# Decoder layer on one Trainium2 core: two output banks for the down projections, and two silus ahead of the turned rows of tile 4

## The chip, the cores and the metric

One Trainium2 chip, one core of it. The metric is the device time of one execution of the whole program in microseconds (us); the time before is the median of three runs. The engines are called PE (TensorE, with PEld for its weight loads), ACT (ScalarE), DVE (VectorE), POOL (GpSimd) and SP (SyncE, which here only issues transfers).

## The reference, cut to what matters

The layer is causal self attention, differential cross attention and a feed-forward part, each behind a layer norm and added to the residual x. The change lies in the last part alone:

```python
def bit_linear(x, w):                      # rows of x in 255 steps, w in three values
    xq = x + stop_gradient(act_quant(x) - x)
    wq = w + stop_gradient(weight_quant(w) - w)
    return einsum('bsd,hd->bsh', xq, wq)
h = bit_linear(x, w1)                      # 128 -> 512
h = depthwise_conv1d(h, conv_w, conv_b)    # 3 taps along the tokens
h = silu(h)
return bit_linear(h, w2)                   # 512 -> 128
```

`act_quant` takes the largest absolute value of a token's row, scales the row to 127 by it, and rounds. So the second `bit_linear` can't begin for a token before the whole row of 512 hidden values is there. x is 2 x 512 tokens of 128 float32 values.

## The kernel before

The 1024 tokens are 8 tiles of 128 (`TT` = 8; four to a batch row). The program is written out by hand, engine by engine: each engine has its own list of instructions, and semaphores carry all order between engines. An engine that stands at a wait holds up all that is behind it in its list.

In the feed-forward part each tile i goes through these steps, each on its engine:

- `conv(i)` on PE (line 984): 10 matmuls of 512 columns, up projection and convolution in one, into one of four banks of PSUM (`CONV_BANK`). A PSUM bank holds 512 float32 values per partition.
- `silu(i)` on ACT (line 665): bank to `hs[:, i % 2]`. It waits for `conv(i)` and, from tile 2 on, until tile i-2 is quantised out of the same half of `hs` (`hq_done`).
- `hidden_scale(i)` on DVE (line 1684): the row's largest value `hmax`, then two small operations to the scale. Three instructions, each waiting for the one before.
- `quantise_hidden(i)` on POOL (line 467) for tiles 0 to 6; for tile 7 `quantise_last` on DVE (line 1693): `hs` times the scale, rounded, into `hq[:, i % 2]`, and then a small operation on the tile's factor `hdq`.
- `turn_hidden(i)` on PE (line 1001): four 128x128 transposes into `HIDDEN_BANK[i % 2]`.
- `turned_hidden(i)` on ACT (line 671): that bank to `hiT[:, i % 2]` in bfloat16. It waits for `turn_hidden(i)` and, from tile 2 on, for `down(i - 2)`, which reads the same half of `hiT`.
- `down(i)` on PE (line 1018): four matmuls of 128 columns into columns 0 to 127 of bank `OB` (bank 7). All eight tiles use this one bank, so `down(i)` waits until `finish(i - 1)` has read it (`f_done` at i).
- `finish(i)` on DVE (line 1702): bank `OB` times `hdq`, plus `x_sb`, into `x_sb`.
- SP (line 285) stores each tile to `out` when it is finished.

The lists around the change, in short. PE (lines 1248 to 1258): ..., `down(1)`, `turn_hidden(2)`, `conv(6)`, `down(2)`, `turn_hidden(3)`, `conv(7)`, `turn_hidden(4)`, `down(3)`, `turn_hidden(5)`, `down(4)`, `turn_hidden(6)`, `down(5)`, `turn_hidden(7)`, `down(6)`, `down(7)`. ACT (lines 712 to 716): `silu(4)`, turned rows of tile 2, `silu(5)`, turned rows 3, `silu(6)`, turned rows 4, `silu(7)`, turned rows 5, 6, 7. DVE (lines 1719 to 1724): `finish(0)`, `hidden_scale(4)`, ..., `finish(3)`, `hidden_scale(7)`, `quantise_last`, `finish(4)`, `finish(5)`, `finish(6)`, `finish(7)`. POOL has the seven `quantise_hidden` in order.

Bank `PJ0` (bank 0) is used earlier in this part for turning the normed tokens; its last reader there is DVE's `low_ints(3, 1, ...)` (line 1716), which counts `xdTl_done` to 3.

In the profile every matmul made by the helper `mm` has line 721. `conv` shows there as `bank<-qk,wqk_h` and the like (the weights lie in `qk`, the tokens in `wqk_h` and `wqk_l`), `down` as `bank<-w_q,pT`, transposes of `turn_hidden` as `bank<-con,onT` at line 1014. `hs` and `hq` show as `onT`, `hiT` as `pT`, because they share that memory.

Of the kernel before, what the change touches and what calls it, by code (L numbers as in the profile page):

```python
# [13 lines left out]
P = 128  # L14
B, T, C = 2, 512, 128
H, DH = 16, 64
NT = T // P
TT = B * NT
# [32 lines left out]
PJ0, SM, PJ1, ST0, ST1, OB = 0, 1, 3, 5, 6, 7  # L51
# [2 lines left out]
VB = (PT, PT + 1, OB)  # L54
CONV_BANK = (PT, PT + 1, SM, SM + 1)
HIDDEN_BANK = (ST0, ST1)
OUT_BANK = (ST1, ST0)
ATT_BANK = (PJ0, OB)

# [21 lines left out]
def decoder_layer(nc, x, consts, wqk, wv, wo, ctxT, xwq, xbq, xwk, xbk, xwv, xbv, xwo, xbo, lam_in,  # L81
                  w1, cw, cb, w2, out):
    with ExitStack() as ctx:
        def sb(name, shape, dt=F32):
            return ctx.enter_context(nc.sbuf_tensor(name, shape, dt))
# [4 lines left out]
        bank = ctx.enter_context(nc.psum_tensor("bank", [P, 8, 512], F32))  # L90


        x_sb = sb("x_sb", [P, TT, C])
# [54 lines left out]
        w2_q = sb("w2_q", [P, FH // P, C], BF16)  # L148
# [10 lines left out]
        hdq = sb("hdq", [P, TT])  # L159
# [40 lines left out]

        xq, cb_row = places(kb_[:, :, :, :].rearrange("p a b c -> p (a b c)"), (NT, C), (FH,))
        _, hiT_f = places(pT_flat, (2, FH // 2), (2, FH // 2))
        hiT, cb_sb = hiT_f.bitcast(BF16), cb_row[0:2]
        qf = onT[:, 6:8, :]
# [15 lines left out]
        def sem_names(*names):  # L220
            return [sem(n) for n in names]
# [27 lines left out]
        wcs, xdTl_done, hq_done, xb_done = sem_names("wcs", "xdTl_done", "hq_done", "xb_done")  # L249
        xd_done, xdT_ps, xdT_done, conv_ps, silu_done, hsc_done, hiT_ps, hiT_done, f_ps, f_done = sem_names(  # L250
            "xd_done", "xdT_ps", "xdT_done", "conv_ps", "silu_done", "hsc_done", "hiT_ps", "hiT_done", "f_ps",
            "f_done")
# [243 lines left out]
        def _(act):  # L496
# [168 lines left out]
            def silu(i):  # L665
                act.wait_ge(conv_ps, i + 1)
                if i >= 2:
                    act.wait_ge(hq_done, i - 1)
                nc.scalar.activation(hs[:, i % 2, :], bank[:, CONV_BANK[i % 4], :], ACT.Silu).then_inc(silu_done, 1)

            def turned_hidden(i):

                act.wait_ge(hiT_ps, i + 1)
                if i >= 2:
                    act.wait_ge(f_ps, i - 1)
                nc.scalar.activation(hiT[:, i % 2, :], bank[:, HIDDEN_BANK[i % 2], :], ACT.Identity,
                                     bias=minus_round[:, :]).then_inc(hiT_done, 1)
# [31 lines left out]
            turned_ints(3, 1, halves[1])  # L709
            silu(3)  # L710
            turned_hidden(1)
            for i in range(4, TT):
                silu(i)
                turned_hidden(i - 2)
            turned_hidden(TT - 2)
            turned_hidden(TT - 1)

        @block.tensor
        def _(pe):
            def mm(out_, lhsT, rhs, start, stop, **kw):  # L720
                return nc.tensor.matmul(out_, lhsT, rhs, start=start, stop=stop, **kw)  # L721
# [249 lines left out]
            def cross_out(at, ts, done):  # L971
                for t in ts:
                    last = mm(bank[:, at, C * t:C * t + C], attT[:, t * P:t * P + P], xwo_sb[:, :], t == ts[0],
                              t == ts[-1], skip_group_check=True)
                last.then_inc(done, 1)
# [8 lines left out]
            def conv(i, taps=range(3)):  # L984

                b, t = i // NT, i % NT
                o = bank[:, CONV_BANK[i % 4], :]
                if taps[0] == 0:
                    pe.wait_ge(xdTl_done, 1 if b == 0 else 2 if t == 0 else 3)
                    if i in (0, 2):  # L990
                        pe.wait_ge(round_done, part_sums + 1 + i // 2)
                    if i >= 4:
                        pe.wait_ge(silu_done, i - 3)
                    mm(o, ones_row[0:2, :], cb_h[0:2], True, False)
                for k in taps:
                    cols = slice(t * P + k, t * P + k + P)
                    last = mm3(o, xdT_h[:, b, cols], xdT_l[:, b, cols], wc_h[:, k, :], wc_l[:, k, :], False, k == 2)
                if taps[-1] == 2:
                    last.then_inc(conv_ps, 1)

            def turn_hidden(i):
# [8 lines left out]
                else:  # L1010
                    pe.wait_ge(hiT_done, i - 1)
                o = bank[:, HIDDEN_BANK[i % 2], :]
                for k in range(FH // P):
# [4 lines left out]
            def down(i):  # L1018
                pe.wait_ge(hiT_done, i + 1)
                if i == 0:  # L1020
                    pe.wait_ge(xo_done, 2)
                else:
                    pe.wait_ge(f_done, i)
                for k in range(FH // P):
                    last = mm(bank[:, OB, 0:C], hiT[:, i % 2, k * P:k * P + P], w2_q[:, k, :], k == 0,
                              k == FH // P - 1)
                last.then_inc(f_ps, 1)

# [206 lines left out]
            pe.wait_ge(attT_done, 2)  # L1235
            cross_out(OUT_BANK[0], first, xo_ps)
            pe.wait_ge(attT_done, 3)
            cross_out(OUT_BANK[1], second, xo_ps)
            conv(1, [1, 2])
# [6 lines left out]
            conv(4, [1, 2])  # L1246
            turn_ints(1, second)
            down(0)
            turn_hidden(1)
            conv(5)  # L1250
            for i in range(6, TT):
                down(i - 5)
                turn_hidden(i - 4)
                conv(i)
            for i in range(TT - 4, TT):
                turn_hidden(i)
                down(i - 1)
# [3 lines left out]
        def _(dve):  # L1261
# [290 lines left out]
            def cross_residual(b, h=0):  # L1552
# [3 lines left out]
                else:  # L1556
                    dve.wait_ge(xo_ps, h + 1)
                    at, ts, n = OUT_BANK[h], range(HALF * h, HALF * h + HALF), HALF
                xs = x_sb[:, NT * b + ts[0]:NT * b + ts[-1] + 1, :]
# [142 lines left out]
            def finish(i):  # L1702
                if i + 1 < TT:
                    dve.wait_ge(hdq_done, i + 1)
                dve.wait_ge(f_ps, i + 1)
                nc.vector.scalar_tensor_tensor(x_sb[:, i, :], bank[:, OB, 0:C], hdq[:, i:i + 1],
                                               x_sb[:, i, :], ALU.mult, ALU.add).then_inc(f_done, 1)

            hidden_scale(0)
# [9 lines left out]
            for i in range(4, TT):  # L1719
                finish(i - 4)  # L1720
                hidden_scale(i)
            quantise_last()
            for i in range(TT - 4, TT):
                finish(i)
# [104 lines left out]
```

## Time and profile before

| | us |
|---|---|
| median of 3 runs | 322.48 |
| the three runs | 322.57, 322.48, 315.58 |
| the profiled execution, its own time | 317.07 |
| its span, first to last instruction | 314.2 |
| time outside the span | 2.87 |
| granted PE clock, mean over the span | 0.989 of full |
| PE busy | 283.5 (90%) |
| DVE busy | 219.8 (70%) |
| ACT busy | 195.1 (62%) |
| POOL busy | 143.1 (46%) |

All positions in time below are us from the start of the span. A row of the timeline gives start, duration, engine, line, operation, what is written and read, and in brackets how long the engine had been idle and what released it. Ends of matmuls are modelled. Engines start an instruction a little before the one in front has drained, so starts can be closer together than durations.

### The profile page before, as it was taken

The page shows a single profiled execution, that of the slowest core. Times are in us where ns is not written, and L with a number is a line of the kernel's source. Part 1 is how long each engine was busy: PE and PEld are TensorE (multiplying, and loading weights), DVE is VectorE, ACT ScalarE, POOL GpSimd, SP SyncE. Part 2 cuts the span into 40 slices and gives each one's busy share as a digit, 9 for nine tenths or more (in the row PEclk, how much of TensorE's full clock was granted, in tenths as well). Part 3 has the DMA queues.
Part 4 walks back from the last instruction along what each step waited for, and adds up shares of the span by engine and source line. Part 5 has one row for each costly group of instructions (what it writes and reads, how often), then busy time and mean ns, then how long its engine had stood idle before and what let it go on. Part 6 is the DMA issues. An engine that isn't in the chain of part 4 may idle for free.

```text
span 314.2 us, 6619 instructions
## 1 busy us (share of the span) xinstructions
PE 283.5 (90%) x2446; PEld 179.3 (57%) x2446; DVE 219.8 (70%) x481; ACT 195.1 (62%) x484; POOL 143.1 (46%) x252
## 2 busy tenths in 40 slices
PE   0899699899999989989899999999999988898893
PEld 0567556566666668656566677445445443355672
DVE  3777767896776642869566747988888689527834
ACT  2588467668777760886677820778867866534333
POOL 3523767794477762565465500086326208001320
PEclk9999889999999999999999999999999999999997
DMA  7920000000000000000000000000000000000001
GB/s 273 306 87 3 0 3 1 2 2 0 3 2 3 2 0 2 0 3 0 2 2 3 2 2 0 2 0 0 2 0 3 1 0 3 0 2 0 8 17 42
DMA packets 4834, 6.16 MB, mean 20 GB/s; under 512 B 834, under 2 KB 3650, under 8 KB 4676
## 3 DMA queue, kind: packets, MB, share of 16 engines
q1 hardware_dynamic: 4516, 5.42, 4.9%
q10 hardware_dynamic: 288, 0.33, 0.4%
q8 instruction: 19, 0.31, 0.4%
q14 instruction: 11, 0.09, 0.1%
HBM read 5.23 MB, written 0.52 MB: 18 GB/s over the span
## 4 chain that ended last, share of the span: by engine, by line
PE 67%; DVE 19%; ACT 7%; issue 5%; DMA 1%; POOL 1%; ACTq 0%; DVEq 0%; POOLq 0%
PE bank L721 58%; PE bank L794 5%; ACT pr L545 4%; DVE nmax L1343 3%; DVE qk L1388 3%; DVE xn L1287 1%; DMA x_sb<-in_x 1%; ACT pT L545 1%; DVE stats L1274 1%; PE bank L946 1%; PE bank L848 1%; DVE qs L1323 1%; PE bank L1014 1%; DVE xn L1669 1%; DVE pT L1359 1%
## 5 line engine op out<-in xcount | busy, mean ns | idle before, releaser
L645 ACT ACTIVATE pT<-bank 128x512 f32<-128x512 f32 (+1 forms) x80 | 44.5, 600 | 25.6 <-PE bank L721 25.1
L338 POOL TENSOR_SCALAR pr<-pr,pinv 128x256 f32<-128x256 f32 (+2 forms) x96 | 45.5, 492 | 29.7 <-DVE pinv L1351 29.6
L1388 DVE TENSOR_REDUCE qk<-bank 128x4 fp32r<-128x616 f32 x64 | 49.0, 796 | 13.6 <-PE bank L721 13.4
L545 ACT ACTIVATE pr<-bank,nmax 128x256 f32<-128x256 f32 (+2 forms) x96 | 44.4, 480 | 18.2 <-DVE nmax L1343 17.9
L721 PE MATMUL bank<-qs 64*128 64x256 f32 (+3 forms) x256 | 50.4, 477 | 4.1 <-ACT pr L545 3.8
L1343 DVE TENSOR_REDUCE nmax<-bank 128x2 f32<-128x512 f32 (+2 forms) x48 | 31.6, 687 | 14.5 <-PE bank L721 14.5
L721 PE MATMUL bank<-pT,v_sb 128*64 128x128 f32 (+2 forms) x320 | 38.4, 385 | 0.0
L338 POOL TENSOR_SCALAR pT<-pT,pinv 128x512 f32<-128x512 f32 x32 | 21.8, 693 | 23.9 <-DVE pinv L1351 23.9
L1359 DVE COPY pT<-bank 128x512 f32<-128x512 f32 (+1 forms) x32 | 30.4, 949 | 1.6 <-PE bank L794 1.5
L721 PEld LDWEIGHTS bank<-pT,v_sb 128*64 128x64 f32 x320 | 21.1, 136 | 14.1 <-issue 10.8
L721 PE MATMUL bank<-km,qk 64*128 64x308 f32 x128 | 27.7, 366 | 1.2 <-DVE qk L1388 1.1
L721 PE MATMUL bank<-qk,km 64*128 64x512 f32 x64 | 27.2, 438 | 1.2 <-ACT pT L645 1.2
L721 PEld LDWEIGHTS bank<-qs 64*128 64x128 f32 x256 | 19.8, 189 | 8.5 <-ACT pr L545 4.3
L348 POOL TENSOR_TENSOR km<-kb_,con 128x1232 fp32r<-128x1232 f32 x8 | 17.9, 2244 | 13.5 <-PE bank L721 13.5
L1351 DVE RECIPROCAL pinv<-psum 128x2 f32<-128x2 f32 x64 | 10.0, 160 | 19.2 <-ACT pT L545 12.8
L721 PEld LDWEIGHTS bank<-mask_b,sel_b 64*128 64x128 bf16 x256 | 13.2, 95 | 17.5 <-issue 13.2
L545 ACT ACTIVATE pT<-bank,nmax 128x512 f32<-128x512 f32 x32 | 22.2, 695 | 1.0 <-DVE nmax L1337 1.0
L556 ACT COPY pT<-bank 128x512 f32<-128x512 f32 x32 | 17.2, 590 | 6.9 <-PE bank L794 6.9
L1337 DVE TENSOR_REDUCE nmax<-bank 128x1 f32<-128x512 f32 x32 | 20.4, 680 | 1.2 <-PE bank L721 1.2
L721 PEld LDWEIGHTS bank<-km,qk 64*128 64x128 f32 x128 | 13.9, 184 | 11.4 <-DVE qk L1388 7.4
L545 ACT ACTIVATION_READ_ACCUMULATOR pr<-bank,nmax 128x1 f32 x96 | 20.2, 211 | 0.0
L473 POOL TENSOR_SCALAR onT<-onT,hscale 128x512 f32<-128x512 f32 x7 | 4.9, 695 | 32.8 <-DVE hscale L1691 26.7
(190 smaller groups left out, 578.9 us busy)
## 6 DMA issues: line engine op xcount, KB each, us to landing
pT<-in_wqk SPq DMA_DIRECT2D x1, 1024.0 KB, 6.3
cw_sb<-in_cw SPq DMA_DIRECT2D x1, 768.0 KB, 8.8
x_sb<-in_x SPq DMA_DIRECT2D x2, 256.0 KB, 5.5
pT<-in_wv SPq DMA_DIRECT2D x1, 512.0 KB, 7.1
wo_sb<-in_wo SPq DMA_DIRECT2D x1, 512.0 KB, 7.3
out<-x_sb SPq DMA_DIRECT2D x8, 64.0 KB, 1.5
onT<-in_consts ACTq DMA_DIRECT2D x1, 256.0 KB, 5.0
pT<-in_xwk SPq DMA_DIRECT2D x1, 256.0 KB, 7.5
```

The lines of the kernel that those rows point to most:

```text
L338: nc.gpsimd.tensor_scalar(d, d, pinv[:, t, a:a + 1], 1.0, ALU.mult, ALU.mult).then_inc(norm_done, 1)
L348: nc.gpsimd.tensor_tensor(km[:, g, :, :], _repeat(kb_[:, g, b, :], GP), _bcast(con[:, C_ROWM:C_ROWM + GP], S2), ALU.mult).then_inc(km_done, 1)
L545: nc.scalar.activation(prob[r][:, a, at:at + w], bank[:, SP[k % 2] + a, at:at + w], ACT.Exp, bias=nmax[:, t, a:a + 1], accum_out=psum[:, t ...
L556: nc.scalar.copy(turned_to(1, 2 * NT)[:, half], bank[:, at, :].rearrange("p (m q) -> p m q", q=64)).then_inc(pt_act, 1)
L645: nc.scalar.activation(px[rows, i, :], bank[rows, (ST0, ST1)[i % 2], :], ACT.Exp, scale=SD ** -0.5).then_inc(xexp_done, 1)
L721: return nc.tensor.matmul(out_, lhsT, rhs, start=start, stop=stop, **kw)
L794: last = nc.tensor.transpose(bank[:, to, at:at + 64], prob[r][own, a, P * i:P * i + P], con[own, C_ID + 64 * half:C_ID + 64 * half + 64])
L1337: nc.vector.tensor_reduce(nmax[:, NT - 1, a:a + 1], bank[:, SP[k % 2] + a, :], AX.X, ALU.max, negate=True).then_inc(max_done, 1)
L1343: nc.vector.tensor_reduce(nmax[:, t, :], bank[:, SP[k % 2]:SP[k % 2] + 2, at:at + w], AX.X, ALU.max, negate=True).then_inc(max_done, 1)
L1351: nc.vector.reciprocal(pinv[:, t, :], psum[:, t, :]).then_inc(inv_done, 1)
L1359: nc.vector.tensor_copy(turned_to(slot, blocks), turned_from(PT, PT + 2, blocks)).then_inc(pt_dve, 1)
L1388: nc.vector.tensor_reduce(m, s_in, AX.X, ALU.max, negate=True).then_inc(round_done, 1)
```

## The change

`down(i)` writes, and `finish(i)` reads, `DOWN_BANK[i % 2]`: bank `OB` for even tiles and bank `PJ0` for odd ones. With two banks `down(i)` waits for `finish(i - 2)` (`f_done` at i - 1) instead of `finish(i - 1)`; `down(1)`, the first in `PJ0`, waits for the bank's last earlier reader (`xdTl_done` at 3). On ACT the last tiles are reordered: `silu(6)` and `silu(7)` are issued one behind the other, and the turned rows of tile 4, which stood between them, come after both. No instruction is added or taken away.

```diff
+DOWN_BANK = (OB, PJ0)
...
-            for i in range(4, TT):
+            for i in range(4, TT - 2):
                 silu(i)
                 turned_hidden(i - 2)
-            turned_hidden(TT - 2)
-            turned_hidden(TT - 1)
+            silu(TT - 2)
+            silu(TT - 1)
+            for i in range(TT - 4, TT):
+                turned_hidden(i)
...
                 pe.wait_ge(hiT_done, i + 1)
                 if i == 0:
                     pe.wait_ge(xo_done, 2)
+                elif i == 1:
+                    pe.wait_ge(xdTl_done, 3)
                 else:
-                    pe.wait_ge(f_done, i)
+                    pe.wait_ge(f_done, i - 1)
                 for k in range(FH // P):
-                    last = mm(bank[:, OB, 0:C], hiT[:, i % 2, k * P:k * P + P], w2_q[:, k, :], k == 0,
+                    last = mm(bank[:, DOWN_BANK[i % 2], 0:C], hiT[:, i % 2, k * P:k * P + P], w2_q[:, k, :], k == 0,
                               k == FH // P - 1)
...
                 dve.wait_ge(f_ps, i + 1)
-                nc.vector.scalar_tensor_tensor(x_sb[:, i, :], bank[:, OB, 0:C], hdq[:, i:i + 1],
+                nc.vector.scalar_tensor_tensor(x_sb[:, i, :], bank[:, DOWN_BANK[i % 2], 0:C], hdq[:, i:i + 1],
                                                x_sb[:, i, :], ALU.mult, ALU.add).then_inc(f_done, 1)
```

ACT's list before, from `silu(4)` (here `onT<-bank`; `pT<-bank,minus_round` are the turned rows, the first of them here tile 2's) to the end of the program:

```order
L669 ACTIVATE onT<-bank 128x512 [waits hq_done,conv_ps]
L676 ACTIVATE pT<-bank,minus_round 128x512 [waits f_ps,hiT_ps]
L669 ACTIVATE onT<-bank 128x512 [waits hq_done,conv_ps]
L676 ACTIVATE pT<-bank,minus_round 128x512 [waits f_ps,hiT_ps]
L669 ACTIVATE onT<-bank 128x512 [waits hq_done,conv_ps]
L676 ACTIVATE pT<-bank,minus_round 128x512 [waits f_ps,hiT_ps]
L669 ACTIVATE onT<-bank 128x512 [waits hq_done,conv_ps]
L676 ACTIVATE pT<-bank,minus_round 128x512 [waits f_ps,hiT_ps] x3
```

And the same list after the change, from `silu(4)` to the end:

```order
L670 ACTIVATE onT<-bank 128x512 [waits hq_done,conv_ps]
L677 ACTIVATE pT<-bank,minus_round 128x512 [waits f_ps,hiT_ps]
L670 ACTIVATE onT<-bank 128x512 [waits hq_done,conv_ps]
L677 ACTIVATE pT<-bank,minus_round 128x512 [waits f_ps,hiT_ps]
L670 ACTIVATE onT<-bank 128x512 [waits hq_done,conv_ps] x2
L677 ACTIVATE pT<-bank,minus_round 128x512 [waits f_ps,hiT_ps] x4
```

`silu(7)` has moved ahead of one instruction, the turned rows of tile 4; everything before and behind stays. The lists of PE, DVE, POOL and SP hold the same instructions in the same order and wait for the same semaphores (but for `down(1)`, which waited for `f_done`); only the values waited for and the bank differ.

## Rows read from the trace of the kernel before

**Rows 1.** The page, granted PE clock in 40 slices, in tenths of full.

```profile
PEclk9999889999999999999999999999999999999997
```

**Rows 2.** Busy time by stretch; the number behind PEld to POOL's is the granted clock.

```profile
302.64:306.00 3.36, 3.36 (x20) 2.67 (x20) 1.09 (x4) 1.29 (x3) 0.93 (x2) 1.00 0.07 20
306.00:310.00 4.00, 2.00 (x22) 1.51 (x19) 2.48 (x8) 2.23 (x4) 0.93 (x2) 1.00 0.06 16
310.00:312.30 2.30, 1.14 (x10) 0.58 (x8) 0.89 (x3) 0.69 (x1) 0.00 (x0) 0.64 0.29 84
```

**Rows 3.** The chain that ended last, in order of time: start, us, what.

```profile
308.85 0.36 DVE x_sb L1706
309.21 0.14 issue
309.34 0.40 PE bank L721 x4
...
309.83 0.36 DVE x_sb L1706
```

**Rows 4.** Timeline of PE from the last matmul of conv(7).

```profile
305.01 0.40 PE L721 MATMUL bank<-qk,wqk_h 128*128 128x512 f32 x1
305.25 0.60 PE L1014 MATMUL bank<-con,onT 128*128 128x128 f32 x4
305.69 0.39 PE L721 MATMUL bank<-w_q,pT 128*128 128x128 bf16 x4
305.91 0.61 PE L1014 MATMUL bank<-con,onT 128*128 128x128 f32 x4
306.68 0.38 PE L721 MATMUL bank<-w_q,pT 128*128 128x128 bf16 x4 [0.16 <-ACT pT L676]
306.90 0.61 PE L1014 MATMUL bank<-con,onT 128*128 128x128 f32 x4
...
309.56 0.61 PE L1014 MATMUL bank<-con,onT 128*128 128x128 f32 x4
...
311.32 0.58 PE L721 MATMUL bank<-w_q,pT 128*128 128x128 bf16 x4 [0.60 <-DVE x_sb L1706]
```

**Rows 5.** Timeline of ACT, same stretch.

```profile
305.89 0.69 ACT L676 ACTIVATE pT<-bank,minus_round 128x512 bf16<-128x512 f32 x1 [1.96 <-PE bank L1014]
306.47 0.59 ACT L669 ACTIVATE onT<-bank 128x512 f32<-128x512 f32 x1
306.95 1.28 ACT L676 ACTIVATE pT<-bank,minus_round 128x512 bf16<-128x512 f32 x2
310.21 0.69 ACT L676 ACTIVATE pT<-bank,minus_round 128x512 bf16<-128x512 f32 x1 [1.98 <-PE bank L1014]
```

**Rows 6.** Timeline of DVE: hidden_scale(4), then the end of the program.

```profile
297.60 0.69 DVE L1687 TENSOR_REDUCE hmax<-onT 128x1 f32<-128x512 f32 x1 [0.28 <-ACT onT L669]
...
306.18 0.35 DVE L1706 SCALAR_TENSOR_TENSOR x_sb<-bank,hdq,x_sb 128x128 f32<-128x128 f32 x1 [1.15 <-PE bank L721]
307.10 0.69 DVE L1687 TENSOR_REDUCE hmax<-onT 128x1 f32<-128x512 f32 x1 [0.56 <-ACT onT L669]
...
308.20 0.49 DVE L1697 TENSOR_SCALAR onT<-onT,hscale 128x512 f32<-128x512 f32 x1
...
311.94 0.35 DVE L1706 SCALAR_TENSOR_TENSOR x_sb<-bank,hdq,x_sb 128x128 f32<-128x128 f32 x1 [0.77 <-PE bank L721]
```

**Rows 7.** Timeline of POOL: tiles 3, 5 and 6 quantised.

```profile
297.15 0.69 POOL L473 TENSOR_SCALAR onT<-onT,hscale 128x512 f32<-128x512 f32 x1
...
302.88 0.69 POOL L473 TENSOR_SCALAR onT<-onT,hscale 128x512 f32<-128x512 f32 x1 [2.44 <-PE bank L1014]
...
306.02 0.69 POOL L473 TENSOR_SCALAR onT<-onT,hscale 128x512 f32<-128x512 f32 x1 [2.20 <-PE bank L1014]
```

**Rows 8.** The page, transfers out: count, KB each, median us to landing.

```profile
out<-x_sb SPq DMA_DIRECT2D x8, 64.0 KB, 1.5
```

## The prediction

> **What bounds the kernel now.** I read the stretches first, then the chain of waits from its end backwards, then the engines' timelines beside it. Up to 306 the feed-forward part is bound by PE: the stretch that holds `conv(7)` is 3.36 us long and PE is busy for all of it at the full clock [rows 2]. Nothing that ACT or DVE does there ends last, so neither half of the change can gain there. From 306.00 to 310.00 PE is busy for 2.00 us of 4.00, and from 310.00 to 312.30 for 1.14 of 2.30 [rows 2]: the end of the program is a chain of short steps that hand over between engines. In that chain stands the pattern this change is about. `finish(4)` runs on DVE at 308.85, PE's `down(5)` starts 0.14 us behind its end, at 309.34, and `finish(5)` follows at 309.83 [rows 3]. The same happens for tiles 6 and 7, up to `down(7)` at 311.32 and `finish(7)` at 311.94 [rows 4, 6]. One bank is written, read, written, read. Worse, `turn_hidden(7)` stands behind `down(5)` in PE's list: its input was quantised at 308.20 + 0.49 = 308.69 [rows 6], yet it starts at 309.56 [rows 4]. What leads to 308.85 is tile 7's own path: `silu(7)` at 306.47 [rows 5], `hmax` of tile 7 at 307.10 and the quantising at 308.20 [rows 6].
>
> **The silus, step by step.** In before, `silu(7)` starts at 306.47, 0.58 behind the turned rows of tile 4 at 305.89, for which ACT had waited 1.96 us [rows 5]. Its own inputs were ready: the last matmul of `conv(7)` runs from 305.01 to 305.41 [rows 4], and tile 5 was quantised out of that half of `hs` by 302.88 + 0.69 = 303.57 [rows 7]. So now `silu(7)` starts at about 305.45, a microsecond earlier, and ends at 306.04. Not all of that counts. DVE's list has `finish(3)` ahead of tile 7's `hmax`, and it starts at 306.18 because `down(3)` stands at 305.69 behind `turn_hidden(4)` [rows 4, 6]; nothing in the change moves it. It lasts 0.35, so `hmax` starts at 306.53 in place of 307.10: 0.57 us gained, with 0.45 of the silu's lead lost to the queue on DVE. If DVE overlaps its drain with the next start, as ACT does, it could be 0.05 to 0.1 more. The following steps keep their distance of 1.10 from `hmax` to quantising [rows 6]: quantising starts at 307.63 and ends at 308.12.
>
> What the moved silu costs: the turned rows of tile 4 stand behind it now. An activation behind a silu starts 0.48 later (306.47 to 306.95, rows 5), so they start at 305.93 instead of 305.89. That is 0.04 late, and `down(4)` with `turn_hidden(6)` move by the same to 306.72 and 306.94 [rows 4]. Had the silu's start been 0.3 later than I think, `down(4)` would be 0.3 later, and still nothing that ends last would be touched, since `turn_hidden(6)` and `down(5)` have until 308.1. POOL's quantising of tile 6 waits for `turn_hidden(4)` and stays at 306.02 [rows 7]. It will now lie beside tile 7's `hmax`. The trace has that pair already: `hmax` of tile 4 at 297.60 took 0.69 with POOL's quantising at 297.15 beside it, and tile 7's at 307.10 took 0.69 with POOL idle [rows 6, 7]. I take nothing for it.
>
> **The banks, step by step.** Until 306 every `down(i)` found `finish(i - 1)` long done, so the looser wait gives nothing. `down(5)` now needs `finish(3)` (done at 306.53) and the turned rows of tile 5 (start 305.93 + 0.58 = 306.51, end about 307.20). It starts right behind `turn_hidden(6)`, 0.44 after it as `down(3)` does behind `turn_hidden(4)` [rows 4]: 307.38, done before 307.8. PE then stands free at `turn_hidden(7)`, which starts when DVE has quantised tile 7. With the 0.14 us that PE took behind DVE [rows 3], that is 308.12 + 0.14 = 308.26. From there by the distances of before: turned rows of tile 7 on ACT 0.65 later (309.56 to 310.21, rows 4 and 5), 308.91; `down(7)` 0.79 behind them (305.89 to 306.68, rows 4 and 5), 309.70; `finish(7)` 0.49 behind that (309.34 to 309.83, rows 3), 310.19. In between nothing is later: `finish(4)` stands 0.65 behind the start of the quantising (308.20 to 308.85, rows 3 and 6), at 308.28, and ends at 308.63; `down(6)` needs that and starts at 308.77; `finish(5)` at about 308.6; `finish(6)` at 309.26 to 309.61. All are out of the way of 309.70.
>
> **The sum.** `finish(7)` at 310.19 in place of 311.94: 1.75 us. Of this the silus alone give 0.57 (the whole chain behind `hmax` shifts). The banks alone give 1.18: quantising ends at 308.69, so 308.83, 309.48, 310.27, 310.76 by the same steps. The four last stores now come at about 0.3, 0.65 and 0.95 us from each other instead of 1 us. A store of 64 KB lands in 1.5 us [rows 8] and the last has its nearest neighbour 0.9 us ahead, so I take the 2.3 us behind `finish(7)` as unchanged; if the transfers did queue, it would cost some tenths. Bounds: PE behind DVE at 0.04 instead of 0.14, `hmax` 0.08 earlier and so on give 1.95. The clock gives the other end. In before it had fallen when `down(7)` ran: 0.64 of full on average in that stretch, and 0.58 us for four matmuls that took 0.38 before [rows 2, 4]. I count the full clock for the new `down(7)`, because it comes at 309.70, before the stretch in which the clock fell; if it is at 1.2 GHz there and in `turn_hidden(7)`, I lose 0.2 to 0.4. So 1.35 to 1.95, with 1.75 taken.
>
> Against the profiled execution: 317.07 - 1.75 = 315.3, or 0.55%. That execution lay near the lowest of the three runs (315.58); the median is 322.48, and the same step from it gives 320.7. The profile does not tell what makes 322 out of 316. About 2% is what a measurement of this kernel can tell from no change, and the three runs alone differ by 7 us, so I expect a real gain that a comparison by 2% calls the same.
>
> **The rivals.** *The silus give nothing* (gain 1.2, 321.3). The ends of matmuls are modelled; if the semaphore of `conv(7)` shows only at about 305.9, or DVE's queue holds tile 7's `hmax` until POOL is through with tile 6's rows at 306.71, the banks' share is left. For it: `silu(7)`'s lead is partly eaten already. Against it: the pair of `hmax` and POOL above.
>
> *The banks give nothing* (gain 0.6, 321.9). That needs something else to hold `turn_hidden(7)` or `down(5)`: the half of `hiT`, or the hidden bank. By rows both are free by 307.3.
>
> *The clock falls in the stage and the kernel ends slower.* PE is the bound until 305.4, and each us of its full-speed work done at 1.2 GHz instead of 2.4 costs up to another us. The clock stands in the highest tenth in every slice from the middle of the program to the last, is at 1.00 up to 310, and fell only at the end, behind a PE that had stood idle from 307.51 to 309.34 and in short pieces since [rows 1 to 4]. If the change made it fall at the first `down` in the second bank, `down(1)`, two rounds of 3.36 us are left up to the end of `conv(7)`: up to 6.7 us more, 1.75 less, so +5.0 and 327.4. It turns the sign from 1.75 us of such work on. Nothing in the rows speaks for it, since PE has the same instructions back to back there and no gap is added. The Trainium skill, page "TensorE: Matmul & The Clock Gate", section "A second HAM failure mode: psum-queue depth-cycling", reports a kernel in which cycling through PSUM banks on each iteration made the engine idle briefly between groups of matmuls and the clock go up and down. By that rule a second bank for `down` could bring this rival about. Convolutions and turned rows here cycle through six banks in that stage already, with the clock at 1.00 [rows 2], so the trace speaks against it here, and I leave it a small chance.
>
> *The measurement lands elsewhere.* If the median falls to the lower of the two levels seen, it reads 315.58 - 1.75 = 313.8, over 2% below 322.48, with the same 1.75 us of real gain.
>
> **How the numbers follow.** Forecast 0.77; silus nothing 0.10; banks nothing 0.05; clock 0.04; other level of the median 0.04. Within 2% are the first three and half of the clock's case, which at +1.6% lies just inside: 0.94. Faster by more is the other level, 0.04; slower by more the other half of the clock's case, 0.02. The range runs from 313.5 (the lowest run less the gain, with its upper bound) to 322.5 (the median without any gain). It is that wide because of the runs, not of the sum; the sum's own range about the median is 320.5 to 321.1.
>
> **What would show it.** Right: `silu(7)` near 305.45 and directly behind it the turned rows of tile 4; tile 7's `hmax` at 306.5 directly behind `finish(3)`; `down(5)` near 307.4 with no wait for DVE; `turn_hidden(7)` released by DVE's quantising at 308.1 to 308.3; `down(7)` released by ACT and not by DVE; span 312.4 to 312.5. Wrong: `down(5)` or `down(6)` still ahead of the path, `hmax` of tile 7 longer than 0.69, or a clock below full before 308.

## The result, and the profile after

| | before | changed |
|---|---|---|
| median of 19 runs, us | 316.62 | 314.47 |
| lowest, us | 315.53 | 313.19 |
| profiled execution, us | 317.07 | 314.22 |
| its span, us | 314.2 | 312.3 |
| PE busy, us | 283.5 | 283.3 |
| first `turn_hidden(4)` to start of `finish(7)`, us | 6.69 | 4.71 |

The ratio is 0.9937, with a 95% interval of 0.991 to 0.9964: some 2.0 us gained (1.1 to 2.8), a real step that is the same kernel by a bound of 2%. Some executions of either kernel (5 of 19 before, 3 of 19 after) take 320 us or more, the changed kernel's at a mean clock of 0.97 instead of 0.98 to 1.00; two of the three runs shown ahead of the prediction were such, and the ratio leaves them out. Of the 2.85 us between the two profiled executions 1.9 lie inside the span; the rest is time outside it (2.87 before, 1.92 after), and no part of what the change does.

The stretches of the changed kernel answer to [rows 2]:

```profile
302.64:306.00 3.36, 3.36 (x21) 2.63 (x20) 1.13 (x4) 1.69 (x4) 0.94 (x2) 1.00 0.07 20
306.00:310.00 4.00, 3.00 (x30) 2.07 (x28) 2.84 (x10) 2.65 (x5) 0.94 (x2) 1.00 0.13 37
310.00:312.30 2.30, 0.00 (x0) 0.00 (x0) 0.35 (x1) 0.00 (x0) 0.00 (x0) 1.00 0.27 78
```

The stage bound by PE is as it was: busy for all of its 3.36 us at clock 1.00. From 306 to 310 PE now does 3.00 us of work instead of 2.00, and behind 310 it has nothing left.

The timeline of PE, against [rows 4]:

```profile
305.29 0.60 PE L1017 MATMUL bank<-con,onT 128*128 128x128 f32 x4
305.72 0.39 PE L724 MATMUL bank<-w_q,pT 128*128 128x128 bf16 x4
305.94 0.61 PE L1017 MATMUL bank<-con,onT 128*128 128x128 f32 x4
306.72 0.40 PE L724 MATMUL bank<-w_q,pT 128*128 128x128 bf16 x4 [0.17 <-ACT pT L677]
306.95 0.61 PE L1017 MATMUL bank<-con,onT 128*128 128x128 f32 x4
307.39 0.39 PE L724 MATMUL bank<-w_q,pT 128*128 128x128 bf16 x4
308.12 0.66 PE L1017 MATMUL bank<-con,onT 128*128 128x128 f32 x4 [0.34 <-DVE onT L1702]
308.73 0.38 PE L724 MATMUL bank<-w_q,pT 128*128 128x128 bf16 x4
309.56 0.40 PE L724 MATMUL bank<-w_q,pT 128*128 128x128 bf16 x4 [0.45 <-ACT pT L677]
```

`down(5)` at 307.39 waits for nothing; before, it stood at 309.34 with 1.84 us of idle PE ahead of it, put down to `finish(4)`:

```profile
309.34 0.38 PE L721 MATMUL bank<-w_q,pT 128*128 128x128 bf16 x4 [1.84 <-DVE x_sb L1706]
```

`turn_hidden(7)` at 308.12 is released by DVE's quantising, and `down(7)` at 309.56 by ACT: no row of PE is released by a finish any more. The timelines of ACT and of DVE, against [rows 5, 6]:

```profile
305.49 0.60 ACT L670 ACTIVATE onT<-bank 128x512 f32<-128x512 f32 x1 [1.52 <-PE bank L724]
305.98 1.30 ACT L677 ACTIVATE pT<-bank,minus_round 128x512 bf16<-128x512 f32 x2
307.59 0.69 ACT L677 ACTIVATE pT<-bank,minus_round 128x512 bf16<-128x512 f32 x1 [0.32 <-PE bank L1017]
308.82 0.69 ACT L677 ACTIVATE pT<-bank,minus_round 128x512 bf16<-128x512 f32 x1 [0.54 <-PE bank L1017]
```

```profile
306.22 0.35 DVE L1711 SCALAR_TENSOR_TENSOR x_sb<-bank,hdq,x_sb 128x128 f32<-128x128 f32 x1 [1.14 <-PE bank L724]
306.48 0.68 DVE L1692 TENSOR_REDUCE hmax<-onT 128x1 f32<-128x512 f32 x1
...
307.58 0.49 DVE L1702 TENSOR_SCALAR onT<-onT,hscale 128x512 f32<-128x512 f32 x1
...
308.23 0.61 DVE L1711 SCALAR_TENSOR_TENSOR x_sb<-bank,hdq,x_sb 128x128 f32<-128x128 f32 x2
...
310.00 0.35 DVE L1711 SCALAR_TENSOR_TENSOR x_sb<-bank,hdq,x_sb 128x128 f32<-128x128 f32 x1 [0.43 <-PE bank L724]
```

`silu(7)` stands at 305.49, directly ahead of the turned rows of tiles 4 and 5. `hmax` of tile 7 has no idle time ahead of it: it starts right behind `finish(3)`. `finish(4)` and `finish(5)` have become one row of two, where [rows 3] had a `down` between them.

### The profile page after: what moved, and what is told of

Same layout as the page of the kernel before. It is cut to its first block, busy times and chain, and to the rows that moved or that the text cites. A ratio compares the mean times of both kernels' runs of the same rounds, so it can differ in the third digit from the quotient of the medians.

```text
span 312.3 us, 6619 instructions
## 1 busy us (share of the span) xinstructions
PE 283.3 (91%) x2446; PEld 179.2 (57%) x2446; DVE 219.7 (70%) x481; ACT 195.2 (63%) x484; POOL 143.5 (46%) x252
## 4 chain that ended last, share of the span: by engine, by line
PE 67%; DVE 18%; ACT 7%; issue 5%; DMA 1%; POOL 1%; ACTq 0%; DVEq 0%; POOLq 0%
PE bank L724 58%; PE bank L797 5%; ACT pr L546 4%; DVE nmax L1348 3%; DVE qk L1393 3%; DVE xn L1292 1%; DMA x_sb<-in_x 1%; ACT pT L546 1%; DVE stats L1279 1%; PE bank L949 1%; PE bank L1017 1%; PE bank L851 1%; DVE qs L1328 1%; DVE xn L1674 1%; DVE pT L1364 1%
```

## The experiments

The part ahead of the tail differs from execution to execution: `turn_hidden(4)` started anywhere from 304.30 to 305.41 in the ten profiles. So spans of single profiles can't be compared to tenths. I compare the tail, which leaves out that part: from the start of `turn_hidden(4)` to the start of `finish(7)`.

### One half of the change at a time

First run: the banks and the looser wait, with ACT's list as before.

```diff
-            for i in range(4, TT - 2):
+            for i in range(4, TT):
                 silu(i)
                 turned_hidden(i - 2)
-            silu(TT - 2)
-            silu(TT - 1)
-            for i in range(TT - 4, TT):
-                turned_hidden(i)
+            turned_hidden(TT - 2)
+            turned_hidden(TT - 1)
```

> Two banks for the down projections and the looser wait, ScalarE's list as before. Theory (the chain as predicted, with the distances of the changed kernel): hmax of tile 7 stays at 307.10 and its quantising at 308.20, but turn_hidden(7) follows it at once at about 308.73 instead of 309.56; from the quantising's start to finish(7) it is 2.42 us as in the changed kernel, so finish(7) at 310.6 and a span of 312.9, 1.3 us below before (314.2). Rival (the banks do nothing, all of the gain is the silus' order): finish(7) at 311.9, span 314.2.

Second run: the kernel before with ACT's new list, one bank and the old wait.

> One bank and the old wait, ScalarE's last two silus ahead of the turned rows of tile 4. Theory: hmax of tile 7 at 306.48 directly behind finish(3), 0.62 earlier than before, the whole ladder of finish and down behind it shifts by that: down(5) at 308.7 behind finish(4), finish(7) at 311.3, span 313.6, a gain of 0.6 us. If the granted clock stays at full there, down(7) takes 0.4 instead of 0.58 and it is 0.8. Rival (the silus' order gives nothing, or gives its whole 1.0 us): span 314.2, or 313.2.

Banks alone, timeline of PE:

```profile
304.30 0.60 PE L1015 MATMUL bank<-con,onT 128*128 128x128 f32 x4
...
306.75 0.40 PE L722 MATMUL bank<-w_q,pT 128*128 128x128 bf16 x4 [0.23 <-ACT pT L677]
307.80 0.66 PE L1015 MATMUL bank<-con,onT 128*128 128x128 f32 x4 [0.66 <-DVE onT L1700]
308.40 0.38 PE L722 MATMUL bank<-w_q,pT 128*128 128x128 bf16 x4
309.23 0.40 PE L722 MATMUL bank<-w_q,pT 128*128 128x128 bf16 x4 [0.45 <-ACT pT L677]
```

Silus alone, timeline of PE:

```profile
304.93 0.60 PE L1016 MATMUL bank<-con,onT 128*128 128x128 f32 x4
...
308.37 0.38 PE L723 MATMUL bank<-w_q,pT 128*128 128x128 bf16 x4 [1.17 <-DVE x_sb L1708]
308.59 0.61 PE L1016 MATMUL bank<-con,onT 128*128 128x128 f32 x4
309.35 0.38 PE L723 MATMUL bank<-w_q,pT 128*128 128x128 bf16 x4 [0.16 <-DVE x_sb L1708]
310.34 0.38 PE L723 MATMUL bank<-w_q,pT 128*128 128x128 bf16 x4 [0.60 <-DVE x_sb L1708]
```

With the banks alone the waits of PE name ACT and the quantising, and no finish; `finish(7)` starts at 309.67, a tail of 5.37 us. With the silus alone the ladder is still there, each `down` released by a finish (`DVE x_sb`), only earlier; `finish(7)` starts at 310.76, a tail of 5.83 us. The two starts of `finish(7)`, from the timelines of DVE, banks alone and silus alone:

```profile
309.67 0.35 DVE L1709 SCALAR_TENSOR_TENSOR x_sb<-bank,hdq,x_sb 128x128 f32<-128x128 f32 x1 [0.43 <-PE bank L722]
310.76 0.35 DVE L1708 SCALAR_TENSOR_TENSOR x_sb<-bank,hdq,x_sb 128x128 f32<-128x128 f32 x1 [0.57 <-PE bank L723]
```

The whole runs agree in order: 0.9955 (0.9941 to 0.9969) for the banks, 0.9974 (0.9952 to 0.9996) for the silus, which lies only just clear of no change. Both halves gain; the rivals by which one does nothing are out.

### Two banks with the old wait

```diff
-                elif i == 1:
-                    pe.wait_ge(xdTl_done, 3)
                 else:
-                    pe.wait_ge(f_done, i - 1)
+                    if i == 1:
+                        pe.wait_ge(xdTl_done, 3)
+                    pe.wait_ge(f_done, i)
```

> The changed kernel with two banks and both silus ahead, but down(i) waits again for finish(i-1). Theory (the wait carries the gain, not the bank that is written beside the one that is read): as the silus alone, finish(7) at 311.3, span 313.6. Rival (a bank of its own speeds the pair of writer and reader by itself): finish(7) near 310.0 and a span near 312.3 as in the changed kernel, or matmuls and finishes shorter than 0.38 and 0.35.

```profile
305.00 0.60 PE L1017 MATMUL bank<-con,onT 128*128 128x128 f32 x4
...
308.44 0.38 PE L724 MATMUL bank<-w_q,pT 128*128 128x128 bf16 x4 [1.17 <-DVE x_sb L1711]
...
310.42 0.58 PE L724 MATMUL bank<-w_q,pT 128*128 128x128 bf16 x4 [0.60 <-DVE x_sb L1711]
```

This timeline of PE has the ladder of the silus alone, number by number: 3.44 us from `turn_hidden(4)` to `down(5)` in both. Its tail is 6.04 us (`finish(7)` at 311.04), 0.21 more than with one bank, and the last row holds that: `down(7)` took 0.58 instead of 0.38, since the granted clock was 0.58 from 310 to 311 in this execution and 1.00 in the other. The finish took 0.35 us in both. So a bank of its own is worth nothing by itself; it is the permission not to wait. The ratio to before is 1.0002 (0.9975 to 1.0029). That holds no change and the expected span of 313.6 alike (0.6 us less, some 0.998), so the whole runs don't show here what the silus still give; but all of the interval lies above the changed kernel's (0.991 to 0.9964).

### The queue on DVE, and the clock

The prediction had the silu's lead partly eaten by `finish(3)`, which stands ahead of tile 7's `hmax` in DVE's list. To move `finish(3)` behind the quantising, `down(5)` must not wait for it. So the last four down projections got the banks that their own tile's convolution had left:

```diff
-DOWN_BANK = (OB, PJ0)
+DOWN_BANK = (OB, PJ0, OB, PJ0, PT, PT + 1, SM, SM + 1)
...
-                else:
+                elif i < 4:
                     pe.wait_ge(f_done, i - 1)
+                else:
+                    pe.wait_ge(silu_done, i + 1)
...
                                         ALU.add).then_inc(hq_last, 1)
+                finish(TT - 5)
...
-            for i in range(4, TT):
+            for i in range(4, TT - 1):
                 finish(i - 4)
                 hidden_scale(i)
+            hidden_scale(TT - 1)
             quantise_last()
```

> On top of the change: the last four down projections each write the bank that their own tile's convolution has left, so that they wait for no finish, and on VectorE finish(3) goes behind the quantising of tile 7. Theory (VectorE's queue eats 0.4 us of the silu's lead): hmax of tile 7 starts behind its silu at 306.12 instead of 306.48, quantising at 307.22, turn_hidden(7) at 307.8 right behind down(5), finish(7) at 309.65, span 311.95, 0.35 us below the changed kernel. Rival (POOL or PE's own queue gates tile 7): hmax earlier but turn_hidden(7) still at 308.1 and the span at 312.3.

Its timeline of DVE:

```profile
305.17 0.69 DVE L1694 TENSOR_REDUCE hmax<-onT 128x1 f32<-128x512 f32 x1 [1.04 <-ACT onT L670]
...
306.27 0.48 DVE L1704 TENSOR_SCALAR onT<-onT,hscale 128x512 f32<-128x512 f32 x1
306.68 0.34 DVE L1714 SCALAR_TENSOR_TENSOR x_sb<-bank,hdq,x_sb 128x128 f32<-128x128 f32 x1
...
308.69 0.35 DVE L1714 SCALAR_TENSOR_TENSOR x_sb<-bank,hdq,x_sb 128x128 f32<-128x128 f32 x1 [0.45 <-PE bank L724]
```

`hmax` is now released by the silu (`ACT onT`) and the finish comes behind the quantising. `turn_hidden(4)` stood at 304.33, so the tail is 4.36 us: 0.35 less than the changed kernel, as expected. The ratio to before is 0.9933 (0.9909 to 0.9958). Four more runs, two of them timed side by side and two of one execution each (own banks, and the kernel before):

> The changed kernel with the last four down projections each in the bank that their own tile's convolution has left, VectorE's list as in the changed kernel. Theory (with two banks no down projection of the tail waits for a finish any more): nothing moves, 4.7 us from the first of turn_hidden(4) to the start of finish(7), as in the changed kernel. Rival (a finish still gates down(5) or down(6)): below 4.6 us.

Tail 4.72 us (305.39 to 310.11), against 4.71 in the changed kernel. Own banks alone move nothing; the 0.35 us are the order on DVE: `hmax` of tile 7 starts 0.84 us behind `turn_hidden(4)` with the late finish, 1.19 in the changed kernel and 1.20 with own banks alone.

> The changed kernel once more, on the same chip as the next run. Theory: 4.7 us from turn_hidden(4) to finish(7), whatever the part ahead of it does; ratio to before 0.993 to 0.995. Rival (the fall of the clock at the end belongs to the kernel before alone): the granted clock stays at 1.00 to the end. By the theory that the clock falls or not from run to run, either can be seen.

> Own banks and finish(3) behind the quantising of tile 7, once more beside the changed kernel. Theory: 4.35 us from turn_hidden(4) to finish(7), 0.35 us less than the changed kernel, so a ratio to before lower by 0.001. Rival: no difference of medians that the rounds can tell, since the part ahead of the tail varies by more.

Tails 4.71 us (304.79 to 309.50) and 4.36 us (305.41 to 309.77): both repeat to 0.01 us. The ratios to before are 0.9895 (0.9845 to 0.9945) and 0.9895 (0.984 to 0.9951): the rounds can't tell the two apart. For the changed kernel 0.993 to 0.995 was expected, so the ratio missed. The medians, 314.17 and 314.32, are where the changed kernel lay before (314.47); what pulls both ratios down and makes the intervals twice as wide is the kernel before in these rounds: the seven executions of it that they rest on are scattered from 315.67 to 319.68. The version with the late finish has the shorter tail in both of its profiles, but in the time of the whole kernel its lead is not shown.

> The kernel before once more. Theory: 6.7 us from turn_hidden(4) to finish(7) if the clock falls again before down(7), 6.5 if it stays at full, since down(7) then takes 0.38 instead of 0.58. Rival (the fall is fixed by the work ahead of it): the clock falls at the same place, near 310.7, in this execution too.

The kernel before, once more, timeline of PE:

```profile
304.95 0.60 PE L1014 MATMUL bank<-con,onT 128*128 128x128 f32 x4
...
309.04 0.38 PE L721 MATMUL bank<-w_q,pT 128*128 128x128 bf16 x4 [1.84 <-DVE x_sb L1706]
...
311.02 0.38 PE L721 MATMUL bank<-w_q,pT 128*128 128x128 bf16 x4 [0.60 <-DVE x_sb L1706]
```

Here the same `down(7)` takes 0.38 us and `finish(7)` starts at 311.44, a tail of 6.49 us. The start of `finish(7)`, from its timeline of DVE:

```profile
311.44 0.35 DVE L1706 SCALAR_TENSOR_TENSOR x_sb<-bank,hdq,x_sb 128x128 f32<-128x128 f32 x1 [0.57 <-PE bank L721]
```

The clock's fall at the end, 0.2 us in [rows 4], belongs to the execution and not to the kernel: PE stood idle for the same 1.84 us in both. The changed kernel's two profiles had it at 1.00 to the end. The late finish had it at 1.00 in one profile, and in the other at 0.68 from 310.00 to 312.30, when PE had ended its work at 309.73 and nothing was lost by it.

All tails together, in us:

| kernel | tail | tail at full clock |
|---|---|---|
| before | 6.69 and 6.49 | 6.49 |
| silus alone | 5.83 | 5.83 |
| two banks, old wait, silus | 6.04 | 5.84 |
| banks alone | 5.37 | 5.37 |
| changed | 4.71 and 4.71 | 4.71 |
| own banks | 4.72 | 4.72 |
| own banks, late finish | 4.36 and 4.36 | 4.36 |

(5.84 is 6.04 less the 0.20 that `down(7)` took longer.) At equal clock the silus give 6.49 - 5.83 = 0.66, the banks 6.49 - 5.37 = 1.12, and both 6.49 - 4.71 = 1.78, which is their sum: they act on two different pieces of one chain. The tail ends at the start of `finish(7)`. From there to the end of the span it is 2.26 to 2.33 us in nine of the ten profiles, and 2.64 with the silus alone, for which I have no cause.

## Why the prediction was right or wrong

**What bounds.** Right. Between the two profiles nothing changed up to 305.4 (`turn_hidden(4)` at 305.25 and 305.29), and the whole gain lies in the tail.

**The silus.** Right in the mechanism and nearly in size: 0.57 forecast, 0.66 measured at equal clock. `silu(7)` started at 305.49 (305.45 forecast) and delayed the turned rows of tile 4 by 0.05 us, measured from `turn_hidden(4)` (0.04 forecast). `hmax` of tile 7 did wait for `finish(3)`, as the 0.35 us of the late finish show. What was mis-sized is the place behind it: I let `hmax` start at the end of the finish, 0.35 behind its start, and it was 0.26 (306.22 to 306.48). The prediction had allowed for 0.05 to 0.1 of this and left it out of the sum.

**The banks.** Right in the mechanism, and 0.14 too small in size. The 1.18 forecast was counted from 311.94, where the profile of before has `down(7)` at the low clock; on that base the banks alone measured 6.69 - 5.37 = 1.32. At full clock the same working gives 0.98, against the 1.12 measured. The old wait with two banks shows the wait to be the cause. `turn_hidden(7)` came 0.05 us behind the quantising's end (307.58 + 0.49 to 308.12), and not 0.14, which was the distance of a `down` behind a finish. `down(7)` behind the turned rows of tile 7 and `finish(7)` behind `down(7)` came 0.05 us sooner each (0.74 and 0.44), the turned rows themselves 0.05 later (0.70).

**The sum.** 1.75 forecast; 1.98 from profile to profile, just above the 1.95 I had as the end, and 1.78 at equal clock. I counted `down(7)` at full clock after the change and at the low clock before, so 0.20 of my 1.75 was a gain of the execution's own and 1.55 was the change. On either base the forecast was short by 0.23: 0.09 at `hmax` and 0.14 in the steps behind the quantising. That 1.75 lies so near to the 1.78 at equal clock is luck. The distance of the last store is as I took it: 2.3 us from `finish(7)` to the end of the span in both. So the span came to 312.3, just under the 312.4 to 312.5 named as a sign.

**The absolute time was wrong.** The step that failed is "the median is 322.48, and the same step from it gives 320.7". The three runs shown were 322.57, 322.48 and 315.58; over 19 runs the median of before is 316.62, and of the changed kernel 314.47. That number is 6.2 us below my number, lies in the range only near its low end, and had I set the number beside the profiled execution, at the 315.3 that the same paragraph works out, it would have been off by 0.8. I had both numbers and four executions, two at 315.58 and 317.07 and two near 322.5; I followed the median where the profile, on which all of the sum rests, lay on the other side. What makes 322 out of 316 stays open: no execution of that length was profiled.

**The rivals.** The silus without effect and the banks without effect are both excluded by the runs with one half alone. The clock that falls in the stage did not come about: 1.00 from 302.64 to 310 in the changed kernel. In the changed kernel the second bank was in use from `down(1)` at 298.54 on, and the granted clock was 1.00 from 280.00 to 306.00. By the section "A second HAM failure mode: psum-queue depth-cycling" of the Trainium skill's "TensorE: Matmul & The Clock Gate", cycling through the banks could have left PE idle between groups and brought the clock down. The trace shows neither: in the stretch of `conv(7)` PE was busy for all of its 3.36 us. The rival by which the measurement lands elsewhere is the one that came about: 313.8 by its working, 314.47 measured. I had it at 0.04, where the three runs shown, one of them near 316, gave it much more.

## What to carry to other kernels

When a writer and a reader on two engines share one buffer, look at what stands behind the writer in its queue: most of the banks' 1.12 us came from `turn_hidden(7)`, which had its data and stood behind a `down` that waited for a finish. With the banks alone it starts 3.50 us behind `turn_hidden(4)` instead of 4.31; the rest comes from `down(7)`, which no longer waits for `finish(6)`. A second buffer gains only through the wait that it lets you drop, so check in the timeline that the wait was there (here for three tiles of eight). When a step is pulled forward, follow it to the next engine's list and see what stands ahead of it there; and forecast an absolute time from the kind of execution that was profiled, not from a median of three that lie 2% apart.

## What the runs showed that I had not expected

- The chain of waits named the wrong releaser. For the changed kernel it runs

```profile
307.11 0.46 PE bank L1017 x4
307.57 0.01 issue
307.58 0.50 DVE onT L1702
```

  as if tile 7's quantising waited for `turn_hidden(6)`. By the code it waits for `hiT_ps` at 6, that is `turn_hidden(5)`, done at 306.55, and for its own scale. The run with the late finish has the quantising at 306.27 while `turn_hidden(6)` runs from 306.00 to 306.60. The two ends were merely 0.01 us apart; a releaser found by its time has to be held against the wait in the code.
- A following step on DVE need not wait for the recorded end of the one in front, and the 0.09 us that this is worth had been left out of the sum: `hmax` starts 0.26 us behind the start of a finish that lasts 0.35.
- The granted clock's falls are not fixed by the program: the same kernels had 0.88 (before, changed) or 1.00 (both once more) from 30 to 40 us, with PE busy for 7.5 of the 10 us in each, and 0.50 (the 1.2 GHz level) or 1.00 during the last `down(7)` of the kernel before. What decides it stays open. Where the clock had fallen from 30 to 40 us, `turn_hidden(4)` started later than in the same kernel's other profile: by 0.30 us in before, 0.50 in the changed kernel and 1.08 with the late finish. That the fall is the whole cause is not shown, since the five profiles without it also range from 304.30 to 304.95.
